# A vision tower on one core: sums of squares by ScalarE's accumulator from a token-major copy of x, all low parts of the expert weights on VectorE, no streaming work on GpSimd

## The reference

```python
# 64 images, 9 patches each: 576 tokens of 4096 values
y = layernorm(patches, ln1_g, ln1_b)      # over 4096 values: mean and variance
y = y @ W_proj + b_proj                   # 4096 -> 192
h = layernorm(y, ln2_g, ln2_b)
xs = layernorm(h)[:, :96]
q = cos(xs) * cos(theta)                  # 12 heads of 8
h = h + softmax(q q^T / sqrt(8)) q @ W_combine.T
xf = layernorm(h)
top_w, top_idx = top-2 softmax of xf @ router_w.T      # 8 experts
for e in range(8):
    h = h + w_e * ((silu(xf @ Wg[e].T) * (xf @ Wu[e].T)) @ Wd[e].T)
```

## Time and profile before

| | |
|---|---|
| median of three runs | 297.85 us |
| span of the profiled execution | 295.3 us |
| what lies around the span, against the median | 2.55 us |
| first expert matmul | 183.17 us |
| VectorE busy | 218.4 us (74%) |
| TensorE busy | 199.8 us (68%) |
| GpSimd busy | 137.1 us (46%) |
| ScalarE busy | 122.2 us (41%) |
| DMA | 39.14 MB |

### The profile page before, as it was taken

The page is one execution under the profiler, slowest core; times in us unless marked ns, Lnnn a source line. Parts: engine busy times, 40 slices in busy tenths (PEclk is TensorE's granted clock), DMA queues, the critical chain, the costliest instruction groups (busy, mean ns, idle before and its releaser), DMA issues.

```text
span 295.3 us, 4727 instructions
## 1 busy us (share of the span) xinstructions
PE 199.8 (68%) x1320; PEld 163.6 (55%) x1333; DVE 218.4 (74%) x522; ACT 122.2 (41%) x265; POOL 137.1 (46%) x150
## 2 busy tenths in 40 slices
PE   0999658297499312837637203999999999999700
PEld 0999647297499301727637102577666666676500
DVE  2599999898899898989898989573555455555404
ACT  0544371380571216847546572343433333343300
POOL 7799992283466164735375687702112111211210
PEclk9999999669598855555555555899999999999965
DMA  6999303999204009526666642231111101111023
GB/s 244 415 338 392 145 0 124 350 389 207 37 2 146 2 10 312 148 82 183 196 208 219 165 133 63 82 89 33 44 44 39 47 31 49 31 47 33 16 87 120
DMA packets 21821, 39.14 MB, mean 133 GB/s; under 512 B 4872, under 2 KB 11560, under 8 KB 21288
## 3 DMA queue, kind: packets, MB, share of 16 engines
q1 hardware_dynamic: 20392, 36.12, 37.8%
q0 software_dynamic: 1408, 2.76, 2.9%
HBM read 33.56 MB, written 5.30 MB: 132 GB/s over the span
## 4 chain that ended last, share of the span: by engine, by line
DVE 53%; PE 31%; DMA 6%; issue 6%; ACT 2%; SPq 2%; DVEq 0%; POOLq 0%; ACTq 0%
DVE rs L695 5%; DVE rs L696 5%; DVE rs L694 4%; PE ps L1191 4%; DVE h L756 4%; PE ps L1189 4%; DMA experts<-w_proj 4%; PE ps L1194 3%; PE ps L1193 3%; DVE experts L345 3%; PE ps L1201 3%; DVE shared L827 3%; PE ps L1190 2%; PE ps L1215 2%; PE ps L1216 2%
## 5 line engine op out<-in xcount | busy, mean ns | idle before, releaser
L1017 PE MATMUL ps<-experts 128*117 128x193 f32 (+1 forms) x320 | 62.7, 359 | 14.0 <-DVE experts L728 7.5
L1017 PEld LDWEIGHTS ps<-experts 128*117 128x117 f32 (+1 forms) x320 | 59.8, 203 | 15.0 <-DMA experts<-x_t 14.6
L345 POOL TENSOR_TENSOR experts<-stage,experts 128x528 bf16<-128x528 f32 x43 | 49.8, 1187 | 37.1 <-ACT experts L520 37.1
L465 POOL TENSOR_TENSOR experts<-experts 128x468 f32<-128x468 f32 x35 | 52.3, 1493 | 26.8 <-ACT experts L506 24.7
L944 DVE TENSOR_TENSOR shared<-shared,ps 128x256 f32<-128x256 f32 x48 | 20.2, 422 | 43.3 <-ACT shared L636 40.4
L487 POOL DMA_INDIRECT pair_y<-shared x16 | 15.6, 972 | 76.1 <-DVE shared L964 55.4
L520 ACT CAST experts<-stage 128x528 f16<-128x528 f32 x64 | 37.6, 628 | 18.2 <-DMA stage<-w_exp 18.0
L636 ACT ACTIVATE shared<-ps 128x256 f32<-128x256 f32 x48 | 18.4, 384 | 56.6 <-PE ps L1194 55.4
L506 ACT ACTIVATE experts<-experts 128x468 f32<-128x468 f32 x40 | 22.8, 590 | 25.9 <-POOL experts L465 18.1
L1215 PE MATMUL ps<-experts,shared 128*128 x96 | 23.6, 246 | 2.0 <-DVE shared L949 1.6
L1216 PE MATMUL ps<-experts,shared 128*128 x96 | 23.6, 246 | 0.0
(11 more groups left out here) (182 smaller groups left out, 379.5 us busy)
## 6 DMA issues: line engine op xcount, KB each, us to landing
stage<-w_exp SPq DMA_DIRECT2D x64, 264.0 KB, 3.3
experts<-x_t SPq DMA_DIRECT2D x4, 1888.0 KB, 13.5
experts<-w_proj SPq DMA_DIRECT2D x4, 768.0 KB, 7.6
shared<-slot_x SPq DMA_DIRECT2D x16, 128.5 KB, 2.1
slot_x<-experts SPq DMA_DIRECT2D x1, 2048.0 KB, 20.4
experts<-x_t SPq DMA_DIRECT2D x4, 472.0 KB, 8.3
yy<-pair_y SPq DMA_DIRECT2D x2, 351.0 KB
out<-h SPq DMA_DIRECT2D x2, 175.5 KB
```

Of the source, the lines that this page charges most:

```text
L345: ops.tensor_tensor(lo_w[:, to + EW:to + EW + PW], stage[:, n % STAGES, :], hi_w[:, to:to + PW], ALU.subtract).then_inc(split_pool if on_p ...
L465: g.tensor_tensor(acc, acc, sq[:, added % 2], ALU.add).then_inc(sq_used, 1)
L1017: last = mm(dst, xbuf[:, t % 2, k, 0:m], gw[:, k, :], start=k == 0, stop=k == KT - 1)
```

## The change

A second copy of x is given as input, `x_rows`, token-major: [5, 117, 4096], a token on a partition. `load_rows(t)` loads tile t of it into one buffer, `rows_in`, once the squares of tile t - 1 are summed. ScalarE squares a whole tile in one instruction of 117x4096 in place, and its accumulator writes the sum of each token into `ssum`, from which `front` reads. The eight-group squares, GpSimd's additions and `square_sum` on TensorE go. GpSimd does no low parts; VectorE does all 64, and a stage buffer is free when `lo_done` says so. `EARLY` is 3 and the raw weight moves to `RAW` = 1 (pieces from 8 on wait for `csum_ready`, pieces from 24 on for the end of the embedding). The order of ScalarE's and VectorE's streams and that of SyncE's loads are rewritten.

```diff
-    EARLY = 4
-    VEC_PIECES = (12, 13, 27, 32, 34, 35, 36, 43, 44, 51, 59, 61, 63)
+    EARLY = 3
+    RAW = 1
...
             def load_x(t):
                 if t >= 2:
                     sp.wait_ge(tok_done, t - 1)
-                    sp.wait_ge(sq_ready, NG * (t - 1))
...
+            def load_rows(t):
+                if t >= 1:
+                    sp.wait_ge(ssum_ready, t)
+                sp.dma_start(rows_in[0:TOK, :], x_rows[t]).then_inc(rows_read, 16)
...
             def load_piece(n):
...
-                    sp.wait_ge(split_pool if on_pool(n - STAGES) else split_vec, splits(n - STAGES))
+                    sp.wait_ge(lo_done, n - STAGES + 1)
...
-            for t in range(TILES):
-                acc = ssq[:, t % 2]
-                for j in range(1, NG):
...
-            for n in range(NP * E):
-                if on_pool(n):
-                    take_rest(pool, g, n)
...
+            def squares(t):
+                sc.wait_ge(rows_read, 16 * (t + 1))
+                a.activation(rows_in[0:TOK, :], rows_in[0:TOK, :], ACT.Square, accum_out=ssum[0:TOK, t:t + 1]).then_inc(ssum_ready, 1)
...
-            rests(0, NP)
             dve.wait_ge(c_bcast, 1)
...
             front(0)
+            rests(0, 7)
             front(1)
-            rests(NP, 14)
+            rests(7, 18)
             front(2)
-            rests(14, 28)
+            rests(18, 22)
             normed(0)
-            rests(28, 33)
             weighed(1)
+            rests(22, 25)
+            normed(1)
+            rests(25, 33)
+            weighed(2)
             rests(33, 37)
-            normed(1)
-            weighed(2)
-            rests(37, 45)
             normed(2)
             low_parts(0)
             low_parts(1)
-            rests(45, 52)
+            rests(37, 43)
             low_parts(2)
             choose()
...
-            rests(52, NP * E)
+            rests(43, NP * E)
...
-            def square_sum(t):
-                pe.wait_ge(ssq_ready, t + 1)
...
-                        for n in (NP * E - 1, NP * E - 2):
-                            pe.wait_ge(split_pool if on_pool(n) else split_vec, splits(n))
+                        pe.wait_ge(lo_done, NP * E)
```

More of the change, by code:

```diff
@@ L5, with vit_tower @@
 from concourse import mybir
-def vit_tower(nc, x, ln1_g, ln1_b, w_proj, b_proj, ln2_g, ln2_b, theta, w_comb, router,
+def vit_tower(nc, x, x_rows, ln1_g, ln1_b, w_proj, b_proj, ln2_g, ln2_b, theta, w_comb, router,
               w_exp, out, slot_x, pair_y):
@@ L65, in vit_tower @@
     RSQRT_SEED = float(0x5F3759DF)
-    EARLY = 4
-    VEC_PIECES = (12, 13, 27, 32, 34, 35, 36, 43, 44, 51, 59, 61, 63)
-    def on_pool(n):
-        return n >= NP and n not in VEC_PIECES
-    def splits(n):
-        return sum(on_pool(i) == on_pool(n) for i in range(n + 1))
+    EARLY = 3
+    RAW = 1
     def spread(ap, dim, n):
@@ L382, in _ @@
             load_x(2)
-            for n in range(STAGES, 9):
-                load_piece(n)
+            load_rows(1)
             load_x(3)
-            for n in range(9, 14):
-                load_piece(n)
+            load_rows(2)
             load_x(4)
+            load_rows(3)
+            load_rows(4)
             sp.wait_ge(pool_consts, 1)
@@ L394, in _ @@
                          allow_slow_non_contiguous=True).then_inc(blank_out, 16)
-            for n in range(14, NP * E):
+            for n in range(STAGES, NP * E):
                 load_piece(n)
@@ L573, in _ @@
             sc.wait_ge(pool_consts, 1)
-            squares(0, 0, NG)
-            squares(1, 0, NG // 2)
-            for j in range(4):
-                squares(1, 4 + j, 5 + j)
-                high_part(j)
-            for j in range(NG):
-                squares(2, j, j + 1)
-                if j == 2:
-                    sc.wait_ge(tok_done, 2)
-                    a.copy(c1_row, ps[ONE_Q:TOKX, emb_at(0):emb_at(0) + D]).then_inc(c1_ready, 1)
-                if j in (0, 1, 5, 6, 7):
-                    high_part(4 + j - (3 if j > 1 else 0))
+            squares(0)
@@ L587, in _ @@
+            high_parts(0, 4)
+            squares(1)
+            high_parts(4, STAGES)
+            sc.wait_ge(tok_done, 2)
+            a.copy(c1_row, ps[ONE_Q:TOKX, emb_at(0):emb_at(0) + D]).then_inc(c1_ready, 1)
             cosine(0, ctheta[0:TOK, :], ang[0:TOK, 0, 0, :])
-            for j in range(NG):
-                squares(3, j, j + 1)
-                if j > 2:
-                    high_part(6 + j)
+            squares(2)
+            squares(3)
             cosine(1, ang[0:TOK, 1, 0:2], ang[0:TOK, 0, 0:2])
-            squares(4, 0, 3)
@@ L683, in rests @@
                 for n in range(n0, n1):
-                    if not on_pool(n):
-                        take_rest(dve, v, n)
+                    take_rest(dve, v, n)
             def rsqrt(var, t0, t1):
@@ L1019, in embed @@
                     last.then_inc(tok_done, 1)
-            def square_sum(t):
-                pe.wait_ge(ssq_ready, t + 1)
-                for i in range(2):
-                    last = mm(ps[0:TOK, ssq_at(t):ssq_at(t) + 1], ssq[:, t % 2, i, :], ones[:, 0:1], start=i == 0, stop=i == 1)
-                last.then_inc(ssq_done, 1)
             def turn_queries(t):
@@ L1102, in _ @@
             embed(2, KT // 2, KT)
-            square_sum(2)
             embed(3, 0, KT)
-            square_sum(3)
             pe.wait_ge(vec_consts, 1)
@@ L1116, in _ @@
             embed(4, 11, KT)
-            square_sum(4)
             weigh(1)
@@ L1278 @@
     full = np.concatenate([full.reshape(TILES, TOK, K), np.ones((TILES, 1, K), tok.dtype)], axis=1)
+    rows = np.ascontiguousarray(full[:, :TOK])
     xt = full.reshape(TILES, TOK + 1, P, KT).transpose(0, 2, 3, 1)
@@ L1288 @@
     ins = {
-        "x_t": xt,
+        "x_t": xt, "x_rows": rows,
         "ln1_g": np.asarray(L0_tok_ln1_g).reshape(P, KT), "ln1_b": np.asarray(L0_tok_ln1_b).reshape(P, KT),
```

84 lines of the change are left out of this document (30 added, 54 removed).

## The result

The changed kernel takes 332.67 us (median of 4 runs, 330.05 to 335.04) against 297.8 for the kernel before on the same chip: ratio 1.114, interval 1.108 to 1.120. Slower was right; the size was not. I had 311 us and a range to 317. The profiled execution is the slowest of the four, 335.04, with a span of 333.3, where the sum of my walk came to 308.3.

What follows compares the result with a forecast made beforehand. VectorE's chain up to the first expert matmul was taken as the bound: 49.8 us of relief against 26.9 of added low parts, plus waits, gave lag 13.0. Added to 297.85: 310.9, rounded to 311 us, range 298 to 317.

Steps and rivals of the forecast that it cites:

- my walk: Stage-by-stage sum of VectorE's work and waits up to the first expert matmul: lag 13.0 us, span 308.3.
- No long small instructions, relief on VectorE: Before the expert stage, without GpSimd's work VectorE's small operations stay short: 49.8 us off, some 50 long operations.
- The start: Up to the broadcast: VectorE free at 38.7, waits 12.4 us, goes on at 51.1; lead 0.8.
- the term of 5.2 us a load: Embedding: each 1.92 MB x_rows tile loads in 5.2 us, between 4.6 at 419 GB/s and 6.3 at 306.
- the landings at 45.0, 55.2 and 68.7: Times in us at which x_rows tiles 1, 2 and 3 were to arrive, each then squared in 3.5 us.
- Rival C: New loads cost more: each 1.1 us later at 306 GB/s, square 4.5; 315 to 319 us, chance 0.14.
- The rule that I weighed and set beside the sum: Loads of 117 rows use 13 DMA engines: 6.4 us each, 2 to 4 us more, 313 to 315.
- The walk behind the landings: From front(0) on: stalls 5.6 and 10.5 us for sines, later waits, lag 13.0 at the first expert matmul.
- the 3.3 us in which piece 7 lands: Before front(1)'s sine: piece 7, issued at 86.3, lands 3.3 us later at 89.6.
- The expert stage unchanged: From the first expert matmul on: same instructions, again 112.1 us, 112 within 1 us.
- The 21 low parts at the end: After choose: 21 low parts where three stood, 13.1 us against 1.9, plus 0.5; first expert matmul at 196.2.
- The square, 3.5 us: ScalarE's square of 4096 values of an x_rows tile, at 0.80 ns a value: 3.5 us.

Runs made afterwards that it cites:

- padded array: Changed kernel with x_rows holding 128 rows a tile in memory, of which each load takes 117; 327.52 us, ratio 1.108.
- all repairs: Changed kernel with 128-row loads, two load buffers, c1 copied first, blanking write behind pieces 7 to 13, scatter words and four low parts early; 294.10 us.
- two buffers alone: Changed kernel with two buffers for the x_rows loads (EARLY 2, RAW 0 for room); 319.59 us, ratio 1.079.

## Why the prediction was wrong in size and right in sign

- **No long small instructions, relief on VectorE:** right. None of 1.1 us stands in VectorE's stream up to the expert stage, and the additions on GpSimd bring them back. I missed one relief, 2.0 us at the end of `front(0)`: the eight copies of the queries took 3.01 us in the kernel before (VectorE's timeline) and 1.04 now (its row at 87.73 above):

```profile
75.25 3.01 DVE L827 COPY shared<-qh 117x192 f16<-117x192 f16 x8
```

- **The start:** VectorE free at 38.3, as forecast (38.7). Broadcast at 57.8, forecast 51.1.
- **The step that failed is the term of 5.2 us a load**, "nearer the first, as both copies of x come in long rows", and with it the landings at 45.0, 55.2 and 68.7. They came at 51.1, 62.8 and 82.6: from first to last packet a load took 10.9, 6.6 and 11.3 us, not 5.2. The earlier trace rows are of loads of 128 partitions on all engines. No row showed one of 117 rows, and a rate was carried over to a shape that it did not belong to: in the run with 128 rows the same three squares start at 44.9, 56.6 and 70.3, close to the forecast. Rival C bounded it from the same rows, so its 315 to 319 was too low for the same reason.
- **The rule that I weighed and set beside the sum** (the Trainium skill, "DMA: Bandwidth & Descriptors", section on why a DMA increments its semaphore by 16: 13 engines for 117 rows) was right, the traces agree with 13 packets in flight; my estimate from it, 2 to 4 us, was not. It counted 16/13 of one load's time. Measured, 117 rows against 128 are 13 us in the changed kernel, as slower packets, uneven ends, and the next load that waits for 13 engines come on top, and each passes through the chain.
- **The walk behind the landings held but for one term, the 3.3 us in which piece 7 lands.** The sine of `front(1)` was late by 17.6 in place of 10.5 because piece 7 was cast at 106.9 in place of some 90. Of these 17 us, 9.3 are its issue (95.6, not 86.3) and 8.0 its landing, 11.3 us in place of 3.3: the median of all pieces did not hold behind the 2 MB of the blanking write. The run with 128 rows shows this term by itself: there piece 7 is issued at 83.1, before the forecast's 86.3, and still cast only at 94.0, and the first expert matmul is 5.0 behind my 196.2. The lag over my walk is 11.9 us at the start of `front(1)` (93.0 against 81.1), 16.4 at that of `front(2)`, 15.8 at `choose`, 18.0 at the first expert matmul: nearly all of it is there by `front(2)`.
- **"The expert stage unchanged" failed** by 7.0 us in the profiled execution, with the sentence that the scatter starts earlier. It starts later, because its words stand behind the last high parts on ScalarE; moved ahead of them, it starts 10.8 us before the first expert matmul.
- **The 21 low parts at the end**, of which I made 13.6 us: the last low parts run from 197.8 to 213.8, 16 us with waits for pieces. Right in place; but in the run without the loads they are there too, and the first expert matmul is only 2.0 behind that of before.
- **The square, 3.5 us:** 3.62, and 0.19 for reading the accumulator, an instruction of its own that I had not counted.

## What to carry to other kernels

A rate taken from the trace belongs to the shape of the transfers that it was taken from. Before a load of an odd number of rows goes into a chain, pad it to 128 or bound it far above the known rate, and look at who shares its engines next. When a load waits for an instruction and the next wait stands behind the load, place cheap and early things (a copy that releases another engine, the loads of the ring) ahead of it in the order. And test repairs together: here six edits that alone were worth 0 to 13 us turned +11% into -1.5%.

## What the runs showed of the hardware that was not expected

- Loads of 16 KB rows, median time of a packet and packets in flight: 128 rows 0.61 us (0.63 in one tile), 16; 117 rows 0.61 to 1.01 in the changed kernel (1.13 and 1.15 in the padded array's first tiles), 13; 112 rows 0.89 to 1.13, 16; 104 rows 1.23 to 1.28, 13. Alone in the queue, 117 rows took no longer than 128 (6.6 and 6.7 us).
- VectorE's wait for GpSimd comes at every second small operation when GpSimd streams without a pause: 1.14 to 1.18 us against 0.16, 65 us in the kernel's time for 139 us of GpSimd work.
- The blanking write of 2048 elements of four bytes holds SyncE for 13.1 us before, 8.5 in the changed kernel, 3.9 with all repairs, and 19.4 with two buffers alone; its size is the same in all of them. A piece issued behind the two blanking writes took 11.3 us to be cast, where the median landing was 3.3.
